# A Mamba-2 block with a gated feed-forward network: decays in two half-chunk buffers, seven of eight W_out tiles in high and low parts, half of the subtractions on ScalarE

## The reference

```
mod = silu(c) @ wmod                       # 6 sections of 512: sa, ca, ga, sb, cb, gb
h   = layernorm(x) * (1 + ca) + sa
z, xBC, dt = split(h @ W_in.T)             # 1024, 1280 and 16 columns
xBC = silu(causal_conv4(xBC)); dt = softplus(dt + dt_bias)
X, B, C = split(xBC)                       # 16 heads of 64, state of 128
Y   = ssd(X, dt * -exp(A_log), B, C)       # per head a decayed scan, chunk by chunk
y   = (Y + D * X) * silu(z)
y   = y * rsqrt(mean(y*y) + 1e-5) * norm_w
x   = x + ga * (y @ W_out.T)
h   = layernorm(x) * (1 + cb) + sb
x   = x + gb * down(silu(gate(h)) * up(h)) # int weights (wq - 128) * scale, hidden 1408
```

## Time and profile before

| what | us |
|---|---|
| median of 3 runs | 1435.08 (1434.65 to 1436.03) |
| profiled execution, its own time | 1434.76 |
| its span, first to last instruction | 1432.9 |
| TensorE busy | 1408.6 (98%) |
| VectorE busy | 1141.1 (80%) |
| ScalarE busy | 642.7 (45%) |
| GpSimd busy | 284.4 (20%) |
| mean granted clock of TensorE | 0.998 of full |

### The profile page before, as it was taken

One profiled execution on the slowest core, in us unless ns is written; L12 is line 12 of the kernel. 1 busy time (PEld: TensorE's weight loads), 2 busy tenths in 40 slices (PEclk: granted clock), 3 DMA queues, 4 the chain that ended last, 5 costly groups with the idle time before them and its releaser, 6 DMA issues.

```text
span 1432.9 us, 25628 instructions
## 1 busy us (share of the span) xinstructions
PE 1408.6 (98%) x9433; PEld 1133.9 (79%) x9433; DVE 1141.1 (80%) x2521; ACT 642.7 (45%) x1300; POOL 284.4 (20%) x335
## 2 busy tenths in 40 slices
PE   7999999999999999999999999899999999999998
PEld 3678787887887887887887887679888888888887
DVE  5799999999999999999999999756646445464542
ACT  5656566566575566576575565322202112120110
POOL 1012222222213213213212212221010211102101
PEclk9999999999999999999999999999999999999999
DMA  9413213213213213123222223612120202202010
GB/s 339 142 52 120 97 39 133 97 38 138 100 46 133 79 56 121 60 95 112 73 91 97 68 104 124 231 45 71 56 88 0 89 22 67 72 18 89 8 52 30
DMA packets 56411, 125.00 MB, mean 87 GB/s; under 512 B 6439, under 2 KB 10067, under 8 KB 52189
## 3 DMA queue, kind: packets, MB, share of 16 engines
q1 hardware_dynamic: 55744, 123.27, 24.2%
q10 hardware_dynamic: 540, 0.07, 0.0%
HBM read 97.62 MB, written 25.69 MB: 86 GB/s over the span
## 4 chain that ended last, share of the span: by engine, by line
PE 87%; issue 5%; DVE 3%; ACT 2%; POOL 1%; DMA 1%; POOLq 0%; SPq 0%; DVEq 0%; ACTq 0%
PE bank L1461 26%; PE bank L2049 18%; PE bank L2079 9%; PE bank L1615 7%; PE bank L1613 6%; PE bank L56 5%; PE bank L1550 4%; PE bank L1578 3%; PE bank L1527 2%; PE bank L1593 2%; PE bank L333 2%; PE bank L1451 1%; PE bank L2030 1%; DVE decay L1069 1%; DVE xBC L994 1%
## 5 line engine op out<-in xcount | busy, mean ns | idle before, releaser
L994 DVE SCALAR_TENSOR_TENSOR xBC<-conv_in,wconv,xBC 128x256 f32<-128x256 f32 x480 | 240.6, 526 | 5.2 <-ACT xBC L709 4.4
L1884 ACT ACTIVATE silu_gate<-bank,params 128x512 f32<-128x512 f32 (+1 forms) x99 | 63.5, 642 | 366.1 <-PE bank L2049 345.2
L1956 DVE SCALAR_TENSOR_TENSOR hidden<-bank,params,silu_gate 128x512 f32<-128x512 f32 (+1 forms) x99 | 68.3, 690 | 125.6 <-PE bank L2049 124.4
L618 POOL TENSOR_TENSOR X_D<-X,Drow 128x1024 f32<-128x1024 f32 x32 | 64.8, 2025 | 390.6 <-ACT X_D L793 318.1
L2079 PE MATMUL bank<-W_down,hidden_high 128*128 128x512 f32 x374 | 138.9, 390 | 0.0
L2049 PE MATMUL bank<-ff_h_high,W_gate 128*128 128x512 f32 (+1 forms) x352 | 132.1, 379 | 0.0
L2049 PE MATMUL bank<-ff_h_high,W_up 128*128 128x512 f32 (+1 forms) x352 | 130.9, 376 | 0.3 <-DVE hidden L1956 0.3
L2049 PE MATMUL bank<-ff_h_low,W_gate 128*128 128x512 f32 (+1 forms) x352 | 130.9, 376 | 0.0
L2049 PE MATMUL bank<-ff_h_low,W_up 128*128 128x512 f32 (+1 forms) x352 | 130.9, 376 | 0.0
L2079 PE MATMUL bank<-W_down,hidden_low 128*128 128x512 f32 x330 | 128.4, 389 | 0.0
L1461 PE MATMUL bank<-h_high,W_in_high 128*128 128x256 f32 x640 | 126.5, 320 | 0.7 <-ACT z_dt L732 0.6
(11 more groups left out here) (194 smaller groups left out, 3230.0 us busy)
## 6 DMA issues: line engine op xcount, KB each, us to landing
decay<-sums_scratch SPq DMA_DIRECT2D x32, 1024.0 KB, 4.8
wq_rows<-wqT SPq DMA_DIRECT2D x33, 256.0 KB, 4.2
widened_scratch<-wq_rows SPq DMA_DIRECT2D x33, 256.0 KB, 2.0
x_tile<-x SPq DMA_DIRECT2D x32, 256.0 KB, 3.0
x_resid<-x SPq DMA_DIRECT2D x32, 256.0 KB, 2.8
x_scratch<-x_resid SPq DMA_DIRECT2D x32, 256.0 KB, 2.3
ff_x_resid<-x_scratch SPq DMA_DIRECT2D x32, 256.0 KB, 4.5
out<-ff_x_resid SPq DMA_DIRECT2D x32, 256.0 KB, 2.0
```

The source lines that it names most:

```text
L618: nc.gpsimd.tensor_tensor(A.XD[:].rearrange("p (h d) -> p h d", h=H), A.X[:].rearrange("p (h d) -> p h d", h=H), A.Drow[:].unsqueeze(2).br ...
L994: nc.vector.scalar_tensor_tensor(A.xc[b][:, m, :], A.raw[:, m, j:j + SC], A.wconv[:, m, j:j + 1], A.xc[b][:, m, :], ALU.mult, ALU.add).the ...
L1956: nc.vector.scalar_tensor_tensor(hid, self.ups[m % 2][:, 0:size], self.T.sup[:, m:m + 1], B.sg[m % 2][:, 0:size], ALU.mult, ALU.mult).then ...
```

## The change

Five things are changed.

1. The two decay buffers hold half of the heads each (`A.L[f]`, 8 heads), and each serves both chunks in turn. The sums of chunk 1 are loaded when `y_diag` of chunk 0 has used the buffer, one turn later than before (`load_sums`), so subtraction, exponential and scores of chunk 1 stand in the turn after, while its chunk 0 is being finished.
2. The memory that this frees goes to W_out: seven tiles are in high and low parts, one stays plain. In the program `KH = KI - 1` takes the place of `KH = KI // 2`. The turned y is split for seven tiles too, so `low_g` and `evac_g` come in two pieces.
3. Subtraction and clamp of the upper eight heads go to ScalarE as relu(s - x), and the exponential then takes scale -1:

```diff
+        def rectify(u, c, q):
+
+            wait(act, cs_in[1], u, 16 * NC, 16 * (c + 1))
+            wait(act, sums_step, u, 3, 3)
+            for h in range(q * HH // 2, (q + 1) * HH // 2):
+                x, g = A.L[1][:, h, :], c * H + HH + h
+                last = nc.scalar.activation(x, x, ACT.Relu, bias=A.s3[:, g:g + 1], scale=-1.0)
+            last.then_inc(rect_done, 1)
...
         def exp_decay(u, c, f):
-            wait(act, diff_done, u, 2 * NC, 2 * c + f + 1)
-            x = A.L[c][:, f * HH:(f + 1) * HH, :]
-            nc.scalar.activation(x, x, ACT.Exp).then_inc(decay_done, 1)
+            wait(act, rect_done if f else diff_done, u, 2 * NC if f else NC, 2 * (c + 1) if f else c + 1)
+            x = A.L[f][:]
+            nc.scalar.activation(x, x, ACT.Exp, scale=-1.0 if f else 1.0).then_inc(decay_done, 1)
+        def load_sums(u, c, f):
+
+            if c:
+                wait(sp, ydiag_done, u, 2 * NC, f + 1)
+            elif u:
+                wait(sp, ydiag_done, before(u), 2 * NC, 2 + f + 1)
+            else:
+
+                sp.wait_ge(setup.wout_low, KH)
+            sp.dma_start(A.L[f][:].rearrange("p h l -> p (h l)"),
+                         T.cs_d[c, f * HH:(f + 1) * HH].rearrange("h l -> (h l)").rearrange("(a x) -> a x", a=1)
+                         .broadcast_to([P, HH * P])).then_inc(cs_in[f], 16)
...
-    KH = KI // 2
+    KH = KI - 1
...
+        def low_g(n, u, c, f):
+
+            ps = t_wait(dve, t_emptied, n, ("g", c, f), 1)
+            k0, k1 = 4 * f, min(4 * f + 4, KH)
+            nc.vector.tensor_tensor(A.gTlo[:, k0:k1, :].rearrange("p k t -> p (k t)"), ps[:, 0:(k1 - k0) * P],
+                                    A.gThi[:, k0:k1, :].rearrange("p k t -> p (k t)").bitcast(F32),
                                     ALU.subtract).then_inc(glo_done, 1)
```

More of the change, by code:

```diff
@@ L542, in turn @@
                 load_resid(u, b, 0)
+            if has_before(n) and n != N:
+                for f in range(2):
+                    load_sums(u, 1, f)
             if n in EXTRA:
@@ L548, in turn @@
                 wait(sp, sums_step, n, 3, 3)
-                for c in range(NC):
-                    wait(sp, cs_in[c], u, 16, 16)
+                for f in range(2):
+                    wait(sp, cs_in[f], u, 16 * NC, 16 * NC)
                 sp.dma_start(T.cs_d.rearrange("c h l -> (c h) l"), A.csT[:]).then_inc(cs_out, 16)
@@ L1062, in diff @@
         def diff(u, c, f):
-            if f == 0:
-                wait(dve, cs_in[c], u, 16, 16)
-                wait(dve, sums_step, u, 3, 3)
-            for h in range(f * HH, (f + 1) * HH):
-                last = nc.vector.tensor_scalar(A.L[c][:, h, :], A.L[c][:, h, :], A.s3[:, c * H + h:c * H + h + 1],
+            wait(dve, cs_in[f], u, 16 * NC, 16 * (c + 1))
+            wait(dve, sums_step, u, 3, 3)
+            for h in range(HH):
+                g = c * H + f * HH + h
+                last = nc.vector.tensor_scalar(A.L[f][:, h, :], A.L[f][:, h, :], A.s3[:, g:g + 1],
                                                0.0, ALU.subtract, ALU.min)
@@ L1196, in first @@
+            softplus(n, 1)
+            setup.gate(dve, 2)
             conv(n, b, 2, 1)
+            softplus(n, 2)
+            softplus(n, 3)
+            softplus(n, 4)
             conv(n, b, 1, 1)
-            softplus(n, 1)
+            softplus(n, 5)
+            softplus(n, 6)
+            conv(n, b, 2, 2)
+            conv(n, b, 4, 0)
             conv(n, b, 1, 2)
-            conv(n, b, 2, 2)
-            softplus(n, 2)
-            setup.gate(dve, 2)
-            softplus(n, 3)
-            setup.low(dve, 4)
@@ L1230, in first @@
             conv(n, b, 5, 2)
             conv(n, b, 7, 0)
+            softplus(n, 12)
+            setup.spread(dve)
+            conv(n, b, 6, 2)
+            conv(n, b, 7, 1)
+            softplus(n, 13)
+            softplus(n, 14)
+            conv(n, b, 7, 2)
             stats(after(n), 0)
-            setup.spread(dve)
             stats(after(n), 1)
+            setup.wout_lo(dve, 0, 4)
+            sums(n)
+            setup.wout_lo(dve, 4, KH)
+            setup.vectors(dve, 4)
             conv(n, b, 8, 0)
-            conv(n, b, 7, 1)
@@ L1247, in first @@
             tails(n, b)
+            split_h(after(n), n, 0)
+            split_h(after(n), n, 1)
+            diff(n, 0, 0)
             setup.scale_gate(dve)
-            diff(n, 0, 0)
-            diff(n, 0, 1)
-            diff(n, 1, 0)
-            diff(n, 1, 1)
-            split_h(after(n), n, 0)
-            setup.wout_lo(dve)
-            split_h(after(n), n, 1)
         def turn(n, b):
@@ L1287, in turn @@
                 softplus(n, 0)
+                softplus(n, 1)
+                conv(n, b, 0, 0)
+            if bef:
+                read_ydiag(n, u, 0, 0)
+            if own:
+                conv(n, b, 0, 1)
+            if bef:
+                read_ydiag(n, u, 0, 1)
+            if own:
+                conv(n, b, 0, 2)
+            if bef:
+                decay_X(n, u, 0)
+                diff(u, 1, 0)
+                gate(n, u, b, 0)
+            if own:
+                softplus(n, 2)
             if bef:
@@ L1445, in transpose_ln @@
                 ps = t_wait(pe, t_emptied, turn_n, ("ln", j), -1)
+                wait(pe, glo_done, before(turn_n), 2 * NC, 2 * NC - 1 + j if turn_n > 0 else 0)
                 for c in range(NC):
@@ L1656, in turn @@
             if bef:
-                scores_G(n, u, b)
+                y_off(u, b, 0, 0)
             if own:
                 project_zdt(n, 0)
+            if bef:
+                scores_G(n, u, b)
+                transpose_x(n, u, b, 0)
+            if own:
                 project_zdt(n, 1)
             if bef:
-                y_off(u, b, 0, 0)
-                transpose_x(n, u, b, 0)
+                transpose_B(n, u, b, 0)
+                y_off(u, b, 0, 1)
             if own:
```

486 lines of the change are left out of this document (243 added, 243 removed).

## The result

The changed kernel takes 1440.32 us (median of 7 runs, 1438.39 to 1443.52), the kernel before 1434.65 on the same chip: ratio 1.0039, 95% interval 1.0029 to 1.0049. It is slower by 5.7 us. The prediction said 1421, and gave "slower" 0.12; the time lies outside its range, too.

What follows compares the result with a forecast made beforehand. TensorE has no gap in a turn and VectorE under 1 us; VectorE's ring sets 53.9. 15 turns x -0.94 = -14.1, drain's output product -1.0, setup 0, hand-over +1.5: -13.6, told as 1421 us, forecast 1416 to 1426, range 1412 to 1436.

Steps and rivals of the forecast that it cites:

- Part 1: TensorE's output product: three more W_out tiles in parts save 0.98 us a turn, 15.6 us in all.
- Part 2: TensorE's new order in a turn: same work, other neighbours, 0.18 and 0.18 us less, so its work is 53.5 us.
- Part 3: VectorE in a turn: work falls from 53.88 to 50.6 us, plus 3.3 of idle, so the turn is 53.9.
- the ring: `read_state`, `y_off`, `scores_G`, `mask_G` wait on each other across turns; 53.9 us, longer than TensorE's 53.5, sets the turn.
- forced idle time of VectorE: Between VectorE's last and first instruction of a turn, ahead of `mask_G`, 3.3 us with nothing to do.
- rival (b): GpSimd's second D·X blocks one more `scores` on VectorE: turn 55.6 us, time 1447; chance 0.12.
- Part 4: ScalarE in a turn: relus, table loads and evacuation pieces raise it from 33.85 to 41.4 us, hidden, at no cost.
- Half a microsecond of slack: In a turn's first half ScalarE empties the fifth tile at 18.7 us; TensorE wants its bank at 19.2.
- rival (a): ScalarE late in a turn's first half through slower relus or later sums, TensorE waits for its bank: 1430; chance 0.15.
- Part 5: Setup and hand-over to the feed-forward network: setup taken as 0, hand-over as +1.5 us.
- the hand-over: From the mixer's drain to the feed-forward network: +1.5 us, range -3 to +5.
- The setup: Start of the kernel: gaps of 60 to 80 us can go (-3.4) or double (+3.4); taken as 0.

Runs made afterwards that it cites:

- e4: The kernel before with the output product alone changed: three more W_out tiles as three products of parts each; 1430.01 us, ratio 0.9961.
- e7: The changed kernel with ScalarE's chunk 1 relus behind evacuations of tiles 3 to 5, and B_rows evacuated ahead of their second half; 1424.69 us, ratio 0.9933.
- e10: e8 without the three products of one W_out tile in each chunk, that tile's share left out; 1405.42 us, ratio 0.9793.
- e2: The changed kernel without the 16 relus a turn; the exponential reads the loaded sums as they are; 1431.01 us, ratio 0.9968.
- e3: The changed kernel with both halves of chunk 1's decay load cut to one head of eight (64 KB for 512 KB); 1422.49 us, ratio 0.9906.
- e5: The changed kernel with steps of its first turn alone put nearer to the order of before, on TensorE and ScalarE; 1436.95 us, ratio 1.0016.
- e13: e11 with the widening of the second block of weight rows moved behind X of turn 1; 1419.98 us, ratio 0.9899.
- e8: The changed kernel with the changes of e5 and e7 together; 1422.63 us, ratio 0.9914.
- e11: e8 with the very first chunk's relus taken from ScalarE, VectorE subtracting and clamping those eight heads too; 1422.20 us, ratio 0.9911.

## Why the prediction was wrong

**Part 1** (0.98 us a turn less for TensorE) stands: 21 products in 4.9 us, a plain tile 0.86. e4 shows that alone it would have brought 0.28.

**Part 2** (another 0.36 from the order) was wrong. With no wait at all (e7) the turn is 53.95; before it was 54.84, less 0.98 is 53.86. The new order gained nothing and cost 0.1. I had priced only the places that got better; which got worse is not worked out, and stays open.

**Part 3** came out at the right number, 53.9, by luck: TensorE's own 53.5 was too low by about as much as the ring was to add. The forced idle time of VectorE is there (3.06 us ahead of `mask_G`; 3.3 were forecast), but its work is 49.2 and not 50.6, and the ring is no ring: "waits for the last `read_state`" is false, since that one belongs to the other sequence. The order of the two in e10 shows it. GpSimd's blocks are there, too: the second `scores` of a turn took 1.65 beside D·X in place of 1.22 (2.92 in the earlier trace rows), and VectorE's gating of one chunk (L1194) 1.94 beside GpSimd's sum in place of 0.96. They reached TensorE nowhere in the changed kernel, whose waits in these turns are all for L726, and rival (b) did not come; e2 shows how near it is.

**Part 4 is the step that failed**: "Half a microsecond of slack: cost nothing". The relus themselves were sized right: four in 1.18 us from start to start, 0.295 each, against 0.28. The Trainium skill (ScalarE: Activation LUTs, section "What ACT_TABLE_LOAD costs") gives an activation with a bias from memory 280 + 0.833 ns per column, less 93 where two follow each other, an estimate of 294 for 128 columns; the trace agrees. The table load was followed by no drain, as forecast (1.28 from 644.88, exponential at 646.18). What was mis-sized is the landing. I scaled it from one load of 1 MB in 4.8 us to 3.6 for 512 KB, and gave each half 3.6, as if they did not share the way. For a half that is alone 3.6 was right (chunk 0's land in 3.6 and 3.8). These two are in flight together: 4.1 and 5.1 in the turn shown, 4.4 and 5.4 in the mean. Counted from that turn's start at 627.92 the second landed at 14.95 and not 13.8, and tile 4 was emptied at 20.0 and not 18.7; TensorE wanted its bank at about 19.3 (I had 19.2). ScalarE itself was late as well, free for the relus at 14.3 and not 13.3, but without the landing that would have been within the slack: up to 4.2 us of landing are free, 0.6 more than I had taken, and the mean is 5.4. From half a microsecond of slack it went to 0.7 us of delay at tile 6 in nearly every turn, and 0 to 1.2 more at tile 5: 1.13 a turn, 16 us. That is rival (a), by its second condition ("the sums land a microsecond later"). I had given it 0.15 and then halved its price, with the argument that something would absorb it. Nothing did: TensorE had no idle time in a turn in which to catch up, so each delay was kept in full, as the turns show that follow the landing one for one. With the landing early (e3) or with less behind it (e7) the forecast's turn of 53.9 is there.

**Part 5**: the hand-over is within its range (564.63 became 563.98 behind the fourteen turns, with four output products at -0.49 each, so about +1.3; +1.5 was forecast). The setup, taken as 0 with a range of 3.4, cost 5.3. Its pieces: the parameters' transposes no longer fill the wait for the first h_low (3.5 us in one piece, in place of 1.46 and 1.12), and in this profile the lower clock then lasts longer (whether by that wait is not shown, see the last section); in turn 1 TensorE waits 2.6 us for X behind relus, exponentials and squares on ScalarE, and 1.4 us of the 5.3 belong to late decays, as e3's second mark shows (103.74 against 105.15). I had written that "the table loads and the exponentials of chunk 0 still stand ahead" and not counted what the diff put beside them. How the 3.4 us that e5 gained divide among the steps it moved stays open.

The prediction had named a turn above 54.5 and a setup more than 3.4 us longer as signs of being wrong; both came.

With both causes mended (e13) the kernel is at 1420.0, where the prediction had put the change. The size of the gain in the turns was right, with the luck of part 3; what it missed was a wait on an engine with 14 us of idle time a turn.

## What to carry to other kernels

An engine that is 60 to 75% busy can still be the one that is waited for: add up its queue in order, from the last moment at which it is surely free, and put the steps that wait for a DMA behind those that free a bank. If the slack that comes out is smaller than the uncertainty of a load's landing, the cost is not zero, and on a bound engine with no gaps a delay is not absorbed but paid in each turn. Where two loads are in flight together, do not give each the time of one alone: here it was 4.4 and 5.4 us in place of 3.6. To find the cause of a turn that varies, set the turns against the landings one by one. Before a wait is called a link of a ring, look at which of two buffers it is for.

## What the runs showed of the hardware that I had not expected

Two loads of 512 KB issued 1.0 us apart landed after 4.1 and 5.1 us (over the turns 3.6 to 4.9 and 4.3 to 6.3), issued 7.8 us apart after 3.6 and 3.8 in the mean; the same upper half in two pieces of 256 KB let ScalarE start early enough to save 11.5 us in all. The Trainium skill (DMA: Bandwidth & Descriptors, section "Rules for kernel authors") says of transfers to disjoint partition halves that they serialize, since both use the same 16 engines. These two halves of heads each go to all 128 partitions, which is another case; the trace shows that together each took longer than one alone.

TensorE's clock after a gap. Setup, 20 to 30 us, before and after, and 80 to 100 after (same columns as above):

```profile
20.00:30.00 10.00, 9.40 (x61) 8.93 (x62) 9.16 (x13) 8.27 (x12) 0.57 (x2) 0.83 1.06 383
```
```profile
20.00:30.00 10.00, 9.41 (x52) 9.08 (x53) 7.45 (x8) 6.86 (x9) 0.13 (x1) 0.66 0.68 240
80.00:100.00 20.00, 19.41 (x173) 15.84 (x173) 16.58 (x44) 13.77 (x31) 1.84 (x1) 0.93 0.20 67
```

A mean of 0.83 over 10 us between the levels of 1.2 and 2.4 GHz is 3.4 us at the lower one; 0.66 is 6.8, and 0.93 over 20 is 2.8. After, each such stretch follows a wait (3.5 us for h_low, 2.6 for X); before, the waits at 18 to 20 us were 1.5 and 1.1, with the parameters' transposes between, and from 80 to 100 the clock was 1.00. In e13, whose wait for X is 1.5, the clock of 60 to 80 and of 80 to 100 is 1.00 again:

```profile
80.00:100.00 20.00, 19.99 (x207) 17.65 (x202) 19.07 (x50) 17.71 (x41) 1.56 (x1) 1.00 0.24 81
```

For the wait for X all profiles agree: behind 2.6 or 3.0 us of it (after, e5, e7, e8, e11) lie 3.2 to 6.8 us at the lower level between 60 and 100, and none in e13. So such a wait is paid more than once. For the earlier stretch they do not: e8 has the two short waits of before and yet means of 0.96 up to 20 and 0.74 from 20 to 30, 6.8 us at the lower level. One profile says little of its length: the mean clock of a whole execution differs between executions of the same kernel, 0.996 to 0.999 before and 0.995 to 0.998 after.
